# Causal attention by head pairs and key pieces, sparse sums by batches of four tiles, query tiles from the longest to the shortest

## The reference

```python
h = tok(x)                          # 16x16 patches of x and four shifted copies, conv, norm, dense
h = concatenate([h, txt], axis=1)   # 8 x 1101 x 128
h = h + attn(layernorm(h))          # 8 heads of 64, causal softmax, W_out, + its own input
h = h + ffn(layernorm(h))

def attn(x):                        # q, k, v of x @ W_in + b_in
    a = softmax(mask(q @ k.T * 64 ** -0.5))
    return (a @ v) @ W_out + b_out + x

def ffn(x):                         # 8 heads of 16, sparse
    x = x + depthwise_conv3(x) + pos_b
    q, k, v = split(x @ qkv_w.T + qkv_b)
    logits = q * 128 ** -0.5 @ k.T
    idx = top_k(logits, 16)         # per row and head
    return softmax(logits at idx) @ (v at idx) @ wo_w.T + wo_b
```

## Time and profile before

| | us |
|---|---|
| median of 3 timed runs | 5693.27 |
| lowest and highest of them | 5663.57, 5711.35 |
| the profiled execution | 5677.68 |
| its span in the profile | 5675.9 |
| mean granted clock of TensorE in it | 0.886 of full |

### The profile page before, as it was taken

One profiled execution on the slowest core, in us unless ns is written; L12 is line 12 of the kernel. 1 busy time (PEld: TensorE's weight loads), 2 busy tenths in 40 slices (PEclk: granted clock), 3 DMA queues, 4 the chain that ended last, 5 costly groups with the idle time before them and its releaser, 6 DMA issues.

```text
span 5675.9 us, 86247 instructions
## 1 busy us (share of the span) xinstructions
PE 4706.9 (83%) x33480; PEld 3201.5 (56%) x33928; DVE 4020.6 (71%) x6958; ACT 2745.6 (48%) x5521; POOL 2101.8 (37%) x1495
## 2 busy tenths in 40 slices
PE   4999699996999779996999879996899869995677
PEld 3666556564566646664666555665565555653444
DVE  1111388875888578884887668884888768884998
ACT  1222255553555445553555445553555535552454
POOL 1000044441444234441444324441444424441565
PEclk8555689997999989998998989998999989997777
DMA  3010300203020210103020030203002030003000
GB/s 51 2 30 0 48 2 3 31 5 50 3 31 1 36 19 3 31 1 53 3 31 1 5 50 3 31 1 52 2 3 31 5 50 3 2 1 50 1 1 5
DMA packets 221474, 103.23 MB, mean 18 GB/s; under 512 B 183616, under 2 KB 198544, under 8 KB 221072
## 3 DMA queue, kind: packets, MB, share of 16 engines
q1 hardware_dynamic: 221072, 97.68, 11.6%
HBM read 78.98 MB, written 18.67 MB: 17 GB/s over the span
## 4 chain that ended last, share of the span: by engine, by line
PE 69%; DVE 10%; ACT 10%; DMA 5%; issue 4%; SPq 2%; POOL 0%; POOLq 0%; ACTq 0%; DVEq 0%
PE causal_ps L600 18%; PE causal_ps L672 14%; PE out_ps L727 13%; PE out_ps L701 7%; PE logit_ps L620 4%; ACT PT L840 4%; DMA H<-in_txt 4%; PE out_ps L709 3%; PE causal_ps L630 2%; ACT split L863 2%; DVE top L1101 2%; DVE A L1126 2%; PE causal_ps L680 1%; DVE top L1121 1%; DVE A L1117 1%
## 5 line engine op out<-in xcount | busy, mean ns | idle before, releaser
L840 ACT ACTIVATE PT<-causal_ps 128x512 f32<-128x512 f32 (+3 forms) x1984 | 1075.9, 569 | 1072.2 <-PE causal_ps L600 1071.8
L510 POOL TENSOR_SCALAR A<-A 128x1101 f32<-128x1101 f32 x576 | 642.2, 1115 | 2493.5 <-DVE A L1126 2493.5
L515 POOL TENSOR_TENSOR A<-A,E 128x1101 f32<-128x1101 f32 x576 | 1377.7, 2392 | 94.2 <-ACT E L893 9.1
L1101 DVE MAX8 top<-logit_ps 128x8 f32<-128x1101 f32 x576 | 754.5, 1310 | 524.4 <-PE logit_ps L620 521.9
L727 PE MATMUL out_ps<-qk,PT 128*128 128x64 f32 x5760 | 852.5, 294 | 27.0 <-ACT PT L840 25.9
L600 PE MATMUL causal_ps<-ident,A 128*128 128x128 f32 (+1 forms) x5184 | 867.4, 299 | 3.6 <-POOL A L515 1.5
L672 PE MATMUL causal_ps<-qk 64*128 64x512 f32 (+3 forms) x1792 | 842.0, 582 | 11.1 <-ACT PB L904 6.6
L727 PEld LDWEIGHTS out_ps<-qk,PT 128*128 128x128 f32 x5760 | 789.4, 211 | 82.8 <-issue 51.7
L701 PE MATMUL out_ps<-PT,Vh 128*32 128x128 f32 (+1 forms) x10368 | 744.6, 294 | 32.6 <-ACT PT L840 10.5
L1121 DVE MAX8 top<-A 128x8 f32<-128x1101 f32 x576 | 753.3, 1308 | 19.7
L1117 DVE MATCH_REPLACE8 A<-top,logit_ps 128x1101 f32<-128x1101 f32 x576 | 746.0, 1295 | 0.3 <-issue 0.2
(11 more groups left out here) (140 smaller groups left out, 3916.9 us busy)
## 6 DMA issues: line engine op xcount, KB each, us to landing
stack<-qk_parts SPq DMA_DIRECT2D x128, 288.0 KB, 19.3
X<-in_x SPq DMA_DIRECT2D x248, 121.5 KB, 4.5
qk_parts<-O SPq DMA_DIRECT2D x16, 864.0 KB, 5.2
Wp<-in_L_attn_W_in SPq DMA_DIRECT2D x96, 64.0 KB, 2.1
out<-OUTB SPq DMA_DIRECT2D x8, 512.0 KB
stack<-in_L_tok_conv_w SPq DMA_DIRECT2D x30, 64.0 KB, 2.4
X<-in_x SPq DMA_DIRECT2D x8, 108.0 KB
H<-in_txt SPq DMA_DIRECT2D x8, 38.5 KB
```

Source lines behind the costliest of these rows:

```text
L510: nc.gpsimd.tensor_scalar(A[:, k % 3, :], A[:, k % 3, :], FAR / -NEG, FAR, ALU.mult, ALU.add).then_inc(marked, 1)
L515: nc.gpsimd.tensor_tensor(A[:, k % 3, :], A[:, k % 3, :], E1[:, k % 2, 0:L], ALU.add).then_inc(chosen, 1)
L840: last = nc.scalar.activation(PT[:, slot, 128 * q0:128 * (q0 + full)], bank[:, 0:128 * full], kept)
L1101: nc.vector.max(top[:, s, 0:8], logit_ps[:, 0:L]).then_inc(top8, 1)
```

## The change

The diff replaces the planner, the causal attention and the sums of the sparse one. What it does:

- **Planner.** `step_events`, `plan` and the numbering are gone. `round_events(sparse, causal)` writes one list per kind of round, for all four pairs at once; a step has one sparse tile and at most one "fill" (a projection or a piece of scores). All five engines go through the same list. Each round ends when its list ends, and nothing is carried over pairs by hand.
- **Order.** `ORDER = list(range(NT))[::-1]`: the query tiles of a pair go from tile 8 (the longest) to tile 0.
- **Causal pieces.** Scores of tile i are cut into pieces of at most 512 keys, and a piece holds both heads of the pair: head 0 on rows 0 to 63 of the array, head 1 on rows 64 to 127, each into a bank of its own. VectorE takes both maxima in one reduction (`rowmax`; later pieces take the minimum with the piece before). ScalarE takes exp of each head, with the maximum known so far. For tiles with several pieces GpSimd computes the difference of maxima (`gap`), ScalarE its exp (`correct`), GpSimd the total (`total`).
- **Scaling.** VectorE inverts the sums (`invert`) and GpSimd scales the weights themselves (`scale`) before they are turned; O is no longer scaled.
- **Causal sums.** V is stationary (64 columns per head) and the turned weights move (128 columns); the output comes transposed, both heads in one 128x128 tile, and ScalarE copies it into OT (`place`). The 36 transposes of O and the copies into OTs before RES are gone, and `("OT", i)` leaves `FILLS`.
- **Sparse sums.** Four sparse tiles are summed together, one in each column group, over all nine key blocks; ScalarE copies the result (`stow`), TensorE turns it back (`return`) and ScalarE writes Os. `split`, `join`, the copies of V into Vh and the division per head are gone; one division serves all heads in `output`.
- **Moved.** The negation of the first maximum goes from VectorE to GpSimd (`negate`). The result is stored from H1; OUTB is gone. The load of the next pair's W_in waits for `proj_v_tail` of the pair before. PB has four slots, PT five, PTc four.

```diff
-FILLS = (tok_order() + ["X1T"] + [("OT", i) for i in range(NT // 3)] + ["RES"] + ["X2T", "FQ", "FK", "FV"])
+FILLS = (tok_order() + ["X1T"] + ["RES"] + ["X2T", "FQ", "FK", "FV"])
...
+BATCH = 4
+SLOTS = BATCH + 1
+PB_SLOTS = 4
+PT_SLOTS = 4
+PER_STEP = 4
+ORDER = list(range(NT))[::-1]
...
+def pieces(i):
+    width = min(128 * (i + 1), L)
+    return [(a, min(a + HALF, width)) for a in range(0, width, HALF)]
+def groups(i):
+    return [[(k, hh) for k in range(i + 1)[2 * g:2 * g + 2] for hh in range(2)] for g in range((i + 2) // 2)]
...
+        if live:
+            ev += [("logits", n), ("pick", n)]
+        if sparse and 1 <= n <= TILES:
+            ev.append(("mark", n - 1))
+        ev += [("total", *u) for u in finishing if len(pieces(u[1])) > 1]
+        if live:
+            ev.append(("negate", n))
+        if sparse and 1 <= n <= TILES:
+            ev.append(("add", n - 1))
...
+        ev += sums[0]
+        if back:
+            ev.append(("turn_sparse", n - 2, 0))
...
+        if fill_now:
+            ev.append(fill_now)
...
+        if live:
+            ev.append(("exp_all", n))
+        ev += [("invert", *u) for u in finishing] + [("scale", *u) for u in finishing]
+        if live:
+            ev.append(("second", n))
+        if back:
+            ev.append(("turn_sparse", n - 2, 1))
+        ev += sums[1]
+        finishing = []
+        if fill_now and fill_now[0] == "scores":
+            ev.append(("rowmax", *fill_now[1:]))
...
+        ev += turns[0:1]
+        if fill_now and fill_now[0] == "scores":
+            ev.append(("exp_part", *fill_now[1:]))
+            _e, p, i, j = fill_now
+            if j == len(pieces(i)) - 1:
+                finishing.append((p, i))
+                ready[p, i] = n + 1
+                if j:
+                    ev += [("gap", p, i), ("correct", p, i)]
+        if live:
+            ev.append(("cut", n))
+        if back:
+            ev.append(("turn_sparse", n - 2, 2))
+        ev += turns[1:]
+        ev += sums[2]
+        if sparse_step(n - 1):
+            ev.append(("return", (n - 3) // BATCH - 1))
...
+                        for hh in range(2):
+                            rows = slice(DK * hh, DK * hh + DK)
+                            last = nc.tensor.matmul(score_v[:, hh, 0:z - a], qk[rows, 0, 128 * i:128 * i + 128],
+                                                    qk[rows, 1, a:z], start=True, stop=not diagonal)
...
+                        for k in range(3 * third, 3 * third + 3):
+                            rows = LAST if k == NT - 1 else 128
+                            for g in range(BATCH):
+                                n = BATCH * b + g
+                                last = nc.tensor.matmul(sums_ps[32 * g:32 * g + 32, :], Vf_of(rows, k, n // NT),
+                                                        PT[0:rows, tile(c, n) % SLOTS, 128 * k:128 * k + 128],
+                                                        start=(k == 0), stop=(k == NT - 1))
...
+                            last = nc.tensor.matmul(sums_ps[half, :], Vp[0:rows, k, half],
+                                                    PTc[0:rows, slot, 128 * q:128 * q + 128],
+                                                    start=(k == 0), stop=(k == i))
```

More of the change, by code:

```diff
@@ L71 @@
 TAIL = L - MAIN
-def blocks(step):
-    return [(t, k, HALF * j + 128 * k) for j, t in enumerate(TILES[step]) for k in range(t % NT + 1)]
+TILES = HF * NT
+BATCH = 4
+SLOTS = BATCH + 1
+PAIR_STEPS = TILES // NP
+PB_SLOTS = 4
+PT_SLOTS = 4
+PER_STEP = 4
+ORDER = list(range(NT))[::-1]
 def fours(items):
@@ L83 @@
 WG = fours(range(NT))
[L86 to L113, removed]
@@ L116, in count_groups @@
[L116 to L135, removed]
@@ L138, in groups_before @@
[L138 to L145, removed]
-def plan(c, p, sparse, causal, carried):
-    first = round_groups(sparse, causal)[0]
-    kind = (sparse, causal, sparse and carried, causal and carried)
-    steps = STEPS
-    if isinstance(p, int) and p == NP:
-        kind, steps = (False, False, sparse, causal), 2
-    at, _end = number_groups(first if carried else 0, steps, *kind)
-    if kind[3]:
-        last, end = number_groups(0, STEPS, sparse, causal, False, False)
-        for event, n, j in list(last):
-            if event == "turn_causal" and n == STEPS - 2:
-                at[event, -2, j] = first + last[event, n, j] - end
-    return steps, kind, at, groups_before(c, p)
+def pieces(i):
+    width = min(128 * (i + 1), L)
+    return [(a, min(a + HALF, width)) for a in range(0, width, HALF)]
@@ new lines, with round_of, number @@
+ROUNDS = {kind: round_events(*kind) for kind in ((False, True), (True, True), (True, False))}
+def round_of(c):
+    return ROUNDS[c > 0, c < B]
+def number(*names):
+    at, n = {}, 0
+    for c in range(B + 1):
+        for e in round_of(c):
+            if e[0] in names:
+                at[(c, *e)] = n
+                n += 1
+        at[c, "end"] = n
+    return at
+TURNS = number("turn_sparse", "turn_causal", "proj_k_tail", "proj_v_tail", "return")
+SCORES = number("proj_q", "proj_k", "proj_v", "scores")
@@ new lines, with tile, batch_of @@
+MAXES = number("rowmax")
+SUMS = number("sum_causal")
+PLACES = number("place", "stow")
+UNITS = number("scale")
+LONG = number("gap")
+LATER = {(c, *e): n for n, (c, e) in enumerate(
+    (c, e) for c in range(B) for e in round_of(c) if e[0] == "rowmax" and e[3] > 0)}
+WIDE = {(c, p, i, j): n for n, (c, p, i, j) in enumerate(
+    (c, *e[1:]) for c in range(B) for e in round_of(c) if e[0] == "scores" and e[3] < 2)}
+def tile(c, t):
+    return (c - 1) * TILES + t
+def batch_of(c, b):
+    return (c - 1) * (TILES // BATCH) + b
@@ L525, in fill_wait @@
+            for c in range(B + 1):
+                if c < B:
+                    halos(c)
+                rounds(c)
         def fill_wait(pe, name, c):
@@ L681, in tensor_event @@
+                        if diagonal:
+                            d = 128 * i - a
+                            for hh in range(2):
+                                last = nc.tensor.matmul(score_v[:, hh, d:z - a], ident_b[:, :], mask_b[:, 0:z - a - d],
                                                         start=False, stop=True)
@@ L913, in projections @@
             def projections(c):
-                for f in range(NT // 3):
-                    acc, free = taken(("OT", f), c)
-                    nc.scalar.copy(OTs[:, 1536 * f:1536 * f + 1536], acc[:, 0:1536]).then_inc(free, 1)
                 seed(c, 2, NT)
```

813 lines of the change are left out of this document (419 added, 394 removed).

## The result

The changed kernel took 5794.07 us (median of 4 runs, 5783.82 to 5810.14), the kernel before 5678.42 beside it: ratio 1.0199, 95% interval 1.0139 to 1.026. The forecast, 5520 us and faster, was wrong in sign; 5794 lies in the range only because it reached up to the rivals. The profiled span is 5783.6 us (before 5675.9).

The account below looks back on a forecast made before the run. The prediction took VectorE to set the mixed rounds and TensorE image 0's. From 5677.7 us it took 125 for image 0's round and 35 for seven mixed rounds: 5518, say 5520, range 5230 to 5830.

Parts of the forecast that it names:

- VectorE's own body term: Mixed round's steps 0 to 70: bare steps, reductions, joins and reciprocals, less filled waits, take VectorE 428 us.
- behind the reciprocal: End of a mixed round: transposes of O and their copies go (4.6 us), one division for all heads costs 1 more.
- 0.05 shows, ... 5.38 us a bare step: VectorE's sparse step: moving the 0.15 us negation to GpSimd shows some 0.05 us, leaving 5.38 us a bare step.
- In the 18 steps ... the next logits therefore stand behind ScalarE: Mixed-round steps with an exponential and three or four causal groups: logits 2.4 us late, 44 us a round in all.
- The projections ... and batches without a gate add 12.5: Mixed-round body: projections and batches of sums in steps without a gate add 12.5 us of waits a round.
- The 25 us for halved clocks and signals: Mixed-round body: 0.35 us a step charged for halved clocks and signals left out, 25 us a round.
- piece by piece ... 33 us: Tail after a mixed round's last MAX8: ten more steps take 33 us, 13.5 more than the old kernel.
- everything at half clock: Image 0's causal round: all priced at half clock, 374 us against 499, a gain of 125.
- (1): Rival: everything but VectorE is covered, gates and projections vanish from the body; 4930 us, chance 0.1.
- (2): Rival: heads don't run together and new array modes cost drains, +26 us a mixed round; 5810 us, chance 0.15.
- (3): Rival: TensorE's clock at 0.77 makes its 350 us 450 to 500, +17 a round over the sum; 5640 us, chance 0.15.
- (4): Rival: ScalarE late in all steps with a piece, 35 more by 0.9 us, +31 a round; 5740 us, chance 0.1.

Follow-up runs that it names:

- E7: Changed kernel with the negation of the maximum back on VectorE, between MAX8 and MATCH_REPLACE8, GpSimd's left out: 5823.53 us, ratio 1.0247 to the kernel before.
- E9: Changed kernel, tiles descending, with only the cut and the third sparse copy moved ahead of the exponentials: 5608.11 us, ratio 0.9884 to the kernel before.
- E3: Changed kernel with exponentials, gap and correction moved behind all causal groups and the third sparse copy: 5532.96 us, ratio 0.976 to the kernel before.
- E5: Changed kernel with the edits of E1 and E3 together: 5298.99 us, ratio 0.9322 to the kernel before.
- E1: Changed kernel with only the order of a pair's query tiles turned, shortest first: 5572.56 us, ratio 0.9837 to the kernel before.
- E11: E5 with the two added 512-column matrix products per sparse step of E4: 5236.09 us, ratio 0.923 to the kernel before.
- E4: Changed kernel with two extra bf16 products of 512 columns per sparse step, overwritten afterwards: 5734.46 us, ratio 1.0113 to the kernel before.

## Why the forecast was wrong, by its own steps

```
term                               forecast   measured   difference
image 0 and all ahead              -125       -171       -46
VectorE's own body term, 7 x       428        437        +66
waits for logits in the body, 7 x  81.5       97.0       +109
tail, 7 x                          33         47.5       +102
behind the reciprocal, 7 x         -3.6       +0.5       +29
last round and end                 0          +7.4       +7
```

The last column sums to 267, and 5520 + 267 = 5787, beside a span of 5783.6. The forecast gave the seven mixed rounds a gain of 35 us, and they lost 271: in the sum, the terms that failed are the waits for logits in steps whose copies stand behind exponentials, the tail, and VectorE's own work. With them the sign was lost, for image 0 gained more than forecast.

**The frame and VectorE.** Right: the reductions took 32.6 + 17.9 = 50.5 us as worked out, the joins 3.5 with 0.8 of gaps. Wrong: "0.05 shows, ... 5.38 us a bare step". Of the 53 bare steps of the last round 50 took 5.44 us or more, so the negation's move saved nothing there (see E7); over 71 steps that is some 4.5 of the 9 us. Reciprocals took 4.7 instead of 2.3, and row maxima waited 3.9 us for scores, which I had named as a sign of a wrong picture. In the step shown above that wait came after TensorE had stood at the start.

**"In the 18 steps ... the next logits therefore stand behind ScalarE": the right mechanism, the wrong size.** 62.6 us against 44. The ten without a batch wait 2.8 us each, near the 2.4 I priced; the eight with a batch 4.3. I had followed the queue behind the exponentials only to the end of the same step. Its other end is the start of the next: the third sparse copy is late there, with it a batch's sums, the sparse transposes and the scores. E9 prices this alone at 22.6 us a round. "The projections ... and batches without a gate add 12.5" measured 34, and E9 explains little of it but the three projections with a batch (9.0, in E9 0.2): the nine without one wait 18.7 us, and 21.4 in E9. Why these were priced too low is open. The 25 us for halved clocks and signals were lumped; the trace can't split them off, since clock and waits move together: in E3 and E5, with fewer waits, it rose from 0.85 to 0.88 and 0.93.

**The tail: "piece by piece ... 33 us" for ten steps.** It was 47.5: 4.8 us a step, where I had priced 3.3. I counted the ten steps and did not ask why there were ten. E1 does: with the order turned it is five, the structure otherwise equal, and the order costs 25.3 us a round there, 177 in all. I never costed the opposite order, though the planner gives the count.

**Behind the reciprocal.** The transposes of O went (4.6 us), and from the reciprocal to the output projections it takes 10.66 us (2495.74 to 2506.40) after 11.36; TensorE's level falls where the tail ends (granted clock 1.00 from 2490 to 2497, 0.57 from 2497 to 2505). Nine transposes and 18 products take the times below, where the trace before has 1.20 and 2.27. The division for all heads costs 1.4 us more, where I had put 1.

```profile
2495.74 0.60 DVE L1178 RECIPROCAL rden<-Os 128x72 f32<-128x72 f32 x1 [3.31 <-ACT PTc L952]
2496.38 1.36 DVE L1180 TENSOR_TENSOR E<-Os,rden 128x1152 f32<-128x1152 f32 x1
...
2497.88 2.15 PE L656 MATMUL logit_ps<-ident,E 128*128 128x128 f32 x9 [1.59 <-DVE E L1180]
...
2501.24 3.71 PE L848 MATMUL causal_ps<-WT,xT 128*128 128x128 f32 x18 [1.21 <-ACT xT L1014]
```

**Image 0: "everything at half clock".** The granted clock was 0.81 there, after 0.55. Of the 46 us more, 37 lie in the round and 9 around it, where the transposes of O are gone too, which I had counted for the mixed rounds alone. Some 10 of the 37 are a slip in my sum: the terms of a pair add to 85 us and not to 87, and 85 makes 364 where I had 374. The rest fits the clock, but no run separates it. Why the new round keeps the upper level with 228 of 337 us busy, where the old one with 458 of 499 did not, no run here tells.

**GpSimd.** Right to take nothing for the small operations: the negation takes 192 ns (L596), not 1.1 us, and in E7, with the negation on VectorE, the logits wait as long as before. GpSimd is busy 330 of 533 us; in the third body VectorE never waits for it and ScalarE once, 1.5 us.

**The rivals.** (1), all covered, is out: even E11's bodies have 48 us of waits. (2), heads in sequence: its time (5810) came nearest and its sign was right, both by luck, for its mechanism was wrong. TensorE in the third round, at the upper clock, after the 1.98 us of the earlier trace rows:

```profile
1935.55 1.13 PE L785 MATMUL causal_ps<-qk 64*128 64x512 f32 x4
```

The heads run side by side: 1.13 us where in sequence it was 1.98, 1.0 forecast. As to drains, in E3's lines above the scores start at 1916.33, where the transposes ahead of them end (1916.34). The Trainium skill, TensorEngine Tiling (Array Packing), Key Properties, states that different tiles execute in parallel, which this agrees with, and that a change of mode drains the array, of which these rows show nothing long enough to price. (3), the clock: 0.86 was granted in the third body and E4 gains 1%, so it bears a part; as a price for itself the 17 us a round is untested, because clock and waits move together. (4), ScalarE late (5740): the nearest in the kind of cause. It was not in 35 more steps, though: these 35, with a piece but no gate, wait 0.4 us together. Nor did ScalarE's work rise to the 380 us a round named for it: it was 304, after 308. It was more in the steps already named, and at the start of the ones after them.

## What to carry to other kernels

With a hand-written order, ask of each instruction in an in-order queue what stands behind it and when that is wanted, and follow it into the next step: a 0.26 us copy behind some 1.4 us of exponentials cost 23 us a round, and swapping them cost nothing in the steps that had logits to serve. A planner's rule (which tile first) is a price: count the steps left when the other work runs out, for both orders, and charge each some 5 us, as here, where little was left to overlap with. Work taken off engines can be eaten by waits: TensorE lost 750 busy us and VectorE 203 while the time rose by 2%, and the same work in a better order (E5) took 6.8% less than the kernel before.

## What the hardware showed that I had not expected

In the mixed bodies TensorE's level fell behind short waits: in the changed kernel's third body it fell 28 times, each time after the engine had stood for 1.1 to 2.7 us, the 2.17 us one above among them, though not after every stand of that length. The scores behind that one took 1.65 us, not 0.92. A body has about 30 stretches of the lower level, 153 to 170 us in all. Idle time is not the whole of it: image 0's round before was busy 458 of 499 us at a clock of 0.55. In the mixed rounds more columns were cheaper than fewer: E4 was 60 us and E11 63 us faster with products whose results nobody reads. And a GpSimd operation on one to four columns takes 0.19 to 0.20 us, not far from VectorE's 0.15.
